# The last layer of a four-layer GNN kernel: where the masks that pick a sender row's chunk are computed

## The reference, cut to what matters

```python
def _L3_gnn_ref(nodes, edges, senders, receivers, ...):
    x = jnp.concatenate([nodes[senders], nodes[receivers], edges], axis=-1)
    h = jax.nn.relu(x @ msg_W1 + msg_b1)
    messages = jax.nn.relu(h @ msg_W2 + msg_b2)
    agg = jax.ops.segment_sum(messages, receivers, num_segments=nodes.shape[0])
    y = jnp.concatenate([nodes, agg], axis=-1)
    y = jax.nn.relu(y @ node_W1 + node_b1) @ node_W2 + node_b2
    ...                       # layer norm of y
    return nodes + y
# reference(): three layers before, then
h = jnp.maximum(_layernorm(x, axis=-1), 0.0)
x = x + _L3_gnn_ref(h, edge_attr_64, src, dst, ...)
```

## Time and profile before

| | us |
|---|---|
| median of 3 runs | 1101.23 |
| lowest and highest of them | 1100.18, 1102.29 |
| the profiled execution | 1098.35 |
| its span, first to last instruction | 1096.6 |
| VectorE busy in it | 827.0 |
| TensorE (matmul) busy in it | 928.3 |
| GpSimd busy in it | 586.4 |

### The profile page before, as it was taken

The page is one execution under the profiler, slowest core; times in us unless marked ns, Lnnn a source line. Parts: engine busy times, 40 slices in busy tenths (PEclk is TensorE's granted clock), DMA queues, the critical chain, the costliest instruction groups (busy, mean ns, idle before and its releaser), DMA issues.

```text
span 1096.6 us, 23929 instructions
## 1 busy us (share of the span) xinstructions
PE 928.3 (85%) x6145; PEld 587.6 (54%) x6145; DVE 827.0 (75%) x2605; ACT 449.9 (41%) x887; POOL 586.4 (53%) x763
## 2 busy tenths in 40 slices
PE   2788888799957868677777968999999999999995
PEld 2465565354535656565563664555555555555553
DVE  8988888743578767778885586768777877777876
ACT  2577777211005444444430143444444344344342
POOL 6534333000016777777740037777777777777770
PEclk9687877799988898999888969999999999999998
DMA  3000000700001111111108036545444454454441
GB/s 65 1 1 0 0 0 0 274 19 1 1 14 37 27 26 27 27 26 27 27 16 264 15 83 169 117 109 107 107 102 108 102 102 107 100 106 107 100 98 39
DMA packets 145112, 72.82 MB, mean 66 GB/s; under 512 B 111917, under 2 KB 136698, under 8 KB 144922
## 3 DMA queue, kind: packets, MB, share of 16 engines
q1 hardware_dynamic: 127224, 54.98, 19.0%
q0 software_dynamic: 16448, 16.88, 8.7%
q10 hardware_dynamic: 1378, 0.22, 0.1%
HBM read 59.66 MB, written 12.35 MB: 66 GB/s over the span
## 4 chain that ended last, share of the span: by engine, by line
PE 36%; POOL 26%; DVE 14%; issue 13%; ACT 4%; DMA 3%; DVEq 2%; ACTq 1%; SPq 0%; POOLq 0%
POOL pair L1208 14%; POOL A L1208 12%; PE seg L1606 12%; PE big L1530 4%; PE seg L1733 4%; ACT A L1343 4%; PE big L1769 3%; PE big L1759 2%; DMA A<-table,src_i 2%; PE seg L1780 2%; PE seg L1801 2%; PE seg L1544 2%; DVE acc_mem L2086 1%; PE big L1587 1%; PE seg L1790 1%
## 5 line engine op out<-in xcount | busy, mean ns | idle before, releaser
L1208 POOL DMA_INDIRECT A<-table,src_i x338 | 321.4, 951 | 116.3 <-issue 97.0
L1208 POOL DMA_INDIRECT pair<-table,src_i x176 | 177.0, 1006 | 67.4 <-issue 53.3
L1343 ACT CAST A<-big 128x500 f32 x208 | 125.4, 603 | 48.1 <-PE big L1535 24.9
L1733 PE MATMUL seg<-A 128*128 128x384 f16 (+1 forms) x624 | 120.1, 336 | 10.6 <-DVE A L1960 8.2
L1769 PE MATMUL big<-A 128*128 128x512 f32 x208 | 109.8, 609 | 1.5 <-DMA A<-pr_table 1.5
L1450 ACT ACTIVATE A<-big,A 128x512 f32<-128x512 f32 x104 | 71.5, 688 | 93.3 <-PE big L1770 93.3
L1444 ACT COPY A<-big 128x512 f32<-128x512 f32 x104 | 60.8, 584 | 118.4 <-PE big L1759 118.4
L1733 PEld LDWEIGHTS seg<-A 128*128 128x128 f16 x624 | 57.0, 98 | 89.1 <-issue 35.2
L1636 PE MATMUL big<-A 128*128 128x300 bf16 x480 | 93.9, 343 | 5.4 <-DVE A L1883 4.8
L1397 ACT ACTIVATE pair<-pair,wcol 128x64 f32<-128x64 f32 x176 | 46.8, 336 | 109.9 <-DMA pair<-table,src_i 109.8
L1271 POOL COPY cur<-pair 128x24 bf16 x100 | 39.7, 439 | 95.5 <-PE seg L1544 95.5
(11 more groups left out here) (306 smaller groups left out, 1770.9 us busy)
## 6 DMA issues: line engine op xcount, KB each, us to landing
A<-in_edge_attr_dram SPq DMA_DIRECT2D x103, 128.0 KB
A<-drel_flat SPq DMA_DIRECT2D x104, 126.0 KB
spilled_adjacency<-A SPq DMA_DIRECT2D x1, 7074.0 KB, 21.9
A<-spilled_adjacency SPq DMA_DIRECT2D x6, 1152.0 KB, 11.7
A<-table,src_i POOLq DMA_INDIRECT x338
A<-pr_table SPq DMA_DIRECT2D x104, 31.5 KB
pair<-table,src_i POOLq DMA_INDIRECT x176
A<-low_flat SPq DMA_DIRECT2D x78, 32.0 KB
```

The costliest lines, as they stand in the source:

```text
L1208: pool.indirect_dma_start(out=row, out_offset=None, in_=table, in_offset=bass.IndirectOffsetOnAxis(ap=src_i[:, tile:tile + 1], axis=0)).th ...
L1343: nc.scalar.copy(A[:, :, bass.ds(bases[k], PW)], big[:, k % 4, 0:PC].rearrange("p (s d) -> p s d", d=PW)).then_inc(window_kept, 1)
L1733: op = nc.tensor.matmul(made[:, 0:held.shape[2] * D], hot_low[:, u, m, :], held[:, k, :, :], start=(m == 0 and k == 0), stop=(m == 3 and k ...
```

## The change

The masks of all 104 groups are computed in one VectorE operation ahead of the loop, behind the signal `pr_ready`: the numbers 0 to 6 against the `src_high` column of tile 2 of each group, 104 x 7 elements a partition (those of group 0 of each pass are computed too and not used). `choose_rows` loses its comparison and the wait for it, and its multiplication reads the group's seven columns of the big mask. `chunk_of` grows from 24 to 728 words a partition, and the tensors carved behind it move up. The semaphore of the comparison falls away.

```diff
--- before.py
+++ after.py
@@ -909,7 +909,7 @@
         h_parts = carve("l3", NC * D).bitcast(F16).rearrange("p (k c f) -> p k c f", k=2, f=D)
         keys = carve("l3", NM * P // 2).bitcast(F16).rearrange("p (u e) -> p u e", u=NM)
         hot_low = carve("l3", NM * 2 * P).bitcast(F16).rearrange("p (u m e) -> p u m e", u=NM, m=4)
-        chunk_of = carve("l3", NM * (HIGH + 1)).rearrange("p (u s) -> p u s", u=NM)[:, :, 0:HIGH]
+        chunk_of = carve("l3", GROUPS * HIGH).rearrange("p (g s) -> p g s", s=HIGH)
         picked = carve("l3", HIGH * D).rearrange("p (s f) -> p s f", f=D)
         iota_4 = carve("l3", 4)
         y1_t = carve("l3", 4 * P)
@@ -1987,12 +1987,9 @@
                     return
                 u = MADE.index(q)
                 m = it * NM + u
-                t = it * (Q * G) + (q * G + 2)
-                dve.tensor_scalar(chunk_of[:, u, :], iota_r[:, 0:HIGH], src_high[:, bass.ds(t, 1)], None, ALU.is_equal).then_inc(ev("chunk_found"), 1)
-                dve.wait_ge(ev("chunk_found"), m + 1)
                 dve.wait_ge(rows_made, m + (NM + 1))
                 dve.tensor_tensor(picked, made.rearrange("p (s f) -> p s f", f=D),
-                                  chunk_of[:, u, :].rearrange("p (s a) -> p s a", a=1).broadcast_to([P, HIGH, D]), ALU.mult).then_inc(ev("picked"), 1)
+                                  chunk_of[:, bass.ds(it * Q + q, 1), :].rearrange("p g s -> p (g s)").rearrange("p (s a) -> p s a", a=1).broadcast_to([P, HIGH, D]), ALU.mult).then_inc(ev("picked"), 1)
                 dve.wait_ge(ev("picked"), m + 1)
                 dve.wait_ge(transposed[q % 2], 1 + 2 * it + q // 2)
                 op = dve.tensor_reduce(X[:, q, 2, 0:D], picked.rearrange("p s f -> p f s"), AX.X, ALU.add)
@@ -2307,6 +2304,8 @@
                     dve.wait_ge(ev("pr_middle"), k)
                     link(dve.tensor_tensor(pr_parts[:, cols, 2, :], pr_rest[:, cols, :], pr_parts[:, cols, 1, :], ALU.subtract))
             dve.sem_inc(ev("pr_ready"), 1)
+            link(dve.tensor_tensor(chunk_of, iota_r[:, 0:HIGH].rearrange("p (a s) -> p a s", a=1).broadcast_to([P, GROUPS, HIGH]),
+                                   src_high.rearrange("p (g j) -> p g j", j=G)[:, :, 2:3].broadcast_to([P, GROUPS, HIGH]), ALU.is_equal))
             dve.wait_ge(ev("chooser_ready"), 1)
             dve.wait_ge(ld_l3, 13 * 16)
 
@@ -2354,7 +2353,7 @@
 
 
 SHARED = {"ld_edges": "rows_weighed", "sum_ps2": "early_steps", "ow_ready0": "pr_high", "ow_ready1": "pr_middle", "ow_ready2": "keys_loaded0", "ow_ready3": "keys_loaded1",
-          "rstd_in": "senders_ready", "rstd_out": "rows_made", "self_out": "rows_chosen", "self_kept": "chunk_found",
+          "rstd_in": "senders_ready", "rstd_out": "rows_made", "self_out": "rows_chosen",
           "neigh_out": "h_parts_ready", "acc_cleared": "rows2_read", "deg_ps": "chooser_ready", "pads": "sums_cleared",
           "sum_ps0": "node_weights_ready", "sum_ps1": "node_steps", "ld_w": "picked", "fills": "rows_16_ready", "h_L2": "src_low_ready", "ld_x": "x_cleared", "sum_ps3": "squares0"}
 
```

## The result

Measured beside each other on one chip, 14 runs each: the changed kernel has a median of 1106.68 us (1102.97 to 1108.2), the kernel before 1102.79 us (1099.52 to 1105.34). The ratio is 1.0036, 95% interval 1.0024 to 1.0047: **slower by 3.9 us**. Predicted were +0.95 us and 1102.2, up to 1105.2 at most. About 1.6 us of the distance is the base: three runs of the kernel before gave 1101.23 us, fourteen gave 1102.79. The rest, 3 us, is the step that failed.

What follows compares the result with a forecast made beforehand. The prediction took GpSimd's gathers to bound the last layer. It added 0.95 us for the new comparison and 0 for everything else to a median of 1101.23 us: 1102.2 us, range 1099.2 to 1105.2.

Steps and rivals of the forecast that it cites:

- The bound: Last layer: paced by GpSimd's 325 gathers, 1.257 us each with gaps, 16.3 us a pass.
- The added comparison: Ahead of the loop on VectorE: 0.95 us, between 0.65 and 1.56, delaying pass 1's gathers; no gather of pass 0 held.
- The removed comparison is worth nothing in the loop: Choice of rows: 0.35 us saved each, 27 us of VectorE time in all, but 0 us off the loop.
- Stretched gathers in the loop: Gathers lengthened by VectorE operations: no net change; bounds -3.3 us and the price of new one-hot collisions.
- the sign of error that I had named: GpSimd's gathers: a mean over 954 ns would show the prediction wrong.
- The price of a collision: A one-hot operation meeting a gather: up to 0.30 us, only if it starts in the last part of a gap.
- The first rival: One-hots of `plain_hots` newly collide with gathers: +4.9 us in all, 1106.1 us; chance 0.15.
- The ring of TensorE and VectorE: Loop: this ring is the bound, waits for chosen rows shrink by 9.8 us, giving 1092.4 us; chance 0.05.
- It costs nothing: Loop's start: the added 0.95 us is absorbed somewhere, giving 1101.2 us; chance 0.09.
- The drain: Behind the last gather: 0 us; a change of more than 0.5 us would show the prediction wrong.

Runs made afterwards that it cites:

- r13: Kernel before with one-hots against PSUM in the loop, from SBUF at their old place in the last pass, and node-weight operations moved into pass 1: ratio 0.9987.
- r3: Changed kernel with the big comparison moved from ahead of the loop into the first `choose_rows`: ratio 1.0027 to the kernel before.
- r2: Kernel before with the big comparison added ahead of the loop into a tile that nothing reads, the loop's own comparisons kept: ratio 1.0006.
- r9: Kernel before with the comparison of each choice of rows and its wait done twice: ratio 1.0039.
- r1: Changed kernel, unaltered, run again for a second profile: ratio 1.0040 to the kernel before.
- r4: Kernel before, unaltered, run again for a second profile: drain 28.32 us, loop 407.82 us.

## Why the prediction was wrong

*The bound: right.* The gathers on GpSimd pace the last layer. The loop without stretch is 404.6 to 404.9 us in all profiles but r13's, where the one wait lies, whatever VectorE did.

*The added comparison: right.* 916 ns were worked out and 916 measured. It held no gather, as it ran from 658.12 to 659.04 us and the gathers beside it started at 657.85 and 659.10. That was its place there: in r3, where it started at 662.34, the gather at 662.52 took 1.54 us. TensorE's wait for the sender one-hots went from 8.2 to 9.1 us. GpSimd's wait is 1.6 us, not 1.95: by the timelines the four transposes behind `make_rows` took 0.84 us instead of 1.06. Start to start it is +0.68 us here and r2's ratio says 0.7, for 0.95 predicted. Two profiles of the kernel before lie 1.05 us apart there, so one profile could not have told.

*The removed comparison is worth nothing in the loop: right as far as it went.* The time saved became waits, as r9 shows from the other side. But "nothing" left out what the saving does to the phase.

*Stretched gathers in the loop:* **the step that failed.** I wrote "I take no net change". It is +3.8 us by the profiles, and the sign of error that I had named came with it: a mean gather of 962 ns, over 954. The argument against, that "a shift breaks old collisions as readily as it makes new ones", takes the phases for evenly spread. They are not: in the kernel before 33 of the 50 one-hots stood behind the endangered stretch, 13 of them at +0.38 us of the fifth gather of their pass and 7 at +0.44 of the twelfth, and only 11 in it. That the shift had far more to lose than to win could have been read from the trace of before. Where the one-hots would land could not be had by taking off the 0.35 us that one choice saves: that gives +0.03 and +0.09, where one-hots held a gather only behind the sender one-hots, and few moved just there. The gathers hold VectorE's operations as well, so the loop settled into other phases, most of them inside the endangered stretch (-0.35 us eight times, -0.27 us twelve times). Which phase a given saving leads to, no run here says ahead of time.

*The price of a collision: mis-sized.* I took 0.30 us as the most and "the last part of a gap" as the condition. Collisions cost up to 0.44 us, and the operation may start anywhere from 0.37 us ahead of the gather, longer than the whole gap, to its start, and behind the sender one-hots to 0.07 us later: 0.37 to 0.44 us of a period of 1.25, 30 to 35%, not a rare chance.

*The first rival* was thus what happened: its mechanism and its place (`plain_hots`). It had 0.15. That its 1106.1 us lies so near 1106.68 is in part luck: it added 4.9 us to a base that the longer series puts 1.6 us higher, and 3.9 were measured.

*The ring of TensorE and VectorE:* excluded by r9 and by the loop's constant length. *It costs nothing:* excluded by the ratio.

*The drain: 0 us, nearly right, with a wrong test.* I named 0.5 us of change there as a sign of error, but the kernel before alone shows 26.46 and 28.32. The change's part is not shown: 0.4 us lie in the open pause, 0.4 us were not placed, and at the lower clock the changed kernel's r1 has a shorter drain than r4.

## What to carry to other kernels

Where a queue of short operations back to back sets the pace, taking work off another engine can't shorten it, but it can shift that engine's operations onto the queue's starts: before such a change, list where each of the neighbour's operations starts against the queue's period and how many stand just clear of a start, and look which of them were themselves held by the queue, for those don't move by what is saved. And where an operation with two SBUF inputs can read one of them from PSUM, try that: here it took the collision away wherever the operation stood. See then to what the moved operation delays at the end of the loop.

## What was not expected of the hardware

- An indirect gather's issue on GpSimd is held by some kinds of VectorE operations and not by others: one-hots with both inputs in SBUF held 10 to 31 gathers in a run of full one-hots; with one input in PSUM none to speak of (28 meetings, 0.09 us). The receivers' comparisons, from 16 bit to 16 bit and with one large input, held gathers too (L2019, 9 of them, 0.8 us in the changed kernel).
- A one-hot that began 0.07 us *after* the gather held it (884.62 and 884.69, 1.39 us instead of 0.94), but only where the sender one-hots ran into it; with the receivers' comparison in front, 25 such starts held none.
- The gathers hold VectorE in turn: receivers' comparisons that began late in a gather ended 0.11 to 0.12 us behind it, and so the two engines' phases are tied.
- The spread of a kernel's runs, some 3 us to either side, has a part that one can name: TensorE's granted clock in the drain is 1.00 in some executions and 0.50 in others of the same kernel (before and r4), and ten matmuls take 2.2 or 4.1 us. A difference between two single profiles has to be cut into stages before it is read.
